# Attention with small batches on one core: scores of a step in one visit, weighted values on quarters of the array, some orders of work changed

## What is computed

```python
W = weights[condition]                                    # per batch element, 32x32
h = einsum('bct,bcd->bdt', x, W)                          # x: (64, 32, 512)
q, k, v = h @ Wq + bq, h @ Wk + bk, h @ Wv + bv           # 512 -> 4096 each
q, k = rms_norm(q, gq), rms_norm(k, gk)                   # over all 4096 columns
attn = softmax(q k^T / sqrt(128))                         # 32 heads of 128, 32 positions
x = x + (attn v) @ Wo + bo                                # 4096 -> 512
...
x = x + ffn(cond2(x))      # a 512x512 quantized weight with a low-rank part, then 8 experts of rank 16
```

## Time and profile before

| what | value |
|---|---|
| median of 3 runs | 1569.63 us (1569.2 to 1571.09) |
| profiled execution | 1569.52 us |
| its span, first to last instruction | 1567.9 us |
| TensorE matmul busy | 1547.8 us, 99% of the span |
| VectorE, ScalarE, GpSimd busy | 1075.9, 709.7, 767.9 us |
| mean granted TensorE clock | 0.997 of full speed |

### The profile page before, as it was taken

How to read it: one execution, slowest core, us unless ns; L and a number is a source line. 1 busy time by engine, 2 the same in 40 slices (tenths; PEclk the granted TensorE clock), 3 DMA queues, 4 the chain that set the end, 5 groups by cost and what they waited for, 6 DMA issues and landing times.

```text
span 1567.9 us, 30891 instructions
## 1 busy us (share of the span) xinstructions
PE 1547.8 (99%) x12566; PEld 1320.7 (84%) x12566; DVE 1075.9 (69%) x1464; ACT 709.7 (45%) x1200; POOL 767.9 (49%) x531
## 2 busy tenths in 40 slices
PE   9999999999999999999999999999999999999998
PEld 8777777777777777777999999998888888888886
DVE  7677677676776767765688888957556655655642
ACT  6666666666666666664333333333332222222210
POOL 6477777777777777764344444424431111111100
PEclk9999999999999999999999999999999999999998
DMA  3111011110011110112333343445452342243220
GB/s 140 55 42 39 26 41 42 42 42 29 34 42 42 42 42 29 35 42 82 120 134 125 134 135 135 145 165 189 155 191 78 89 134 89 93 135 94 81 94 27
DMA packets 105885, 134.33 MB, mean 86 GB/s; under 512 B 6016, under 2 KB 88064, under 8 KB 105232
## 3 DMA queue, kind: packets, MB, share of 16 engines
q1 hardware_dynamic: 105280, 132.23, 25.5%
q10 hardware_dynamic: 464, 0.13, 0.0%
HBM read 86.20 MB, written 46.14 MB: 84 GB/s over the span
## 4 chain that ended last, share of the span: by engine, by line
PE 88%; POOL 4%; DVE 4%; issue 3%; ACT 1%; DMA 1%; POOLq 0%; SPq 0%; DVEq 0%; ACTq 0%
PE bank L558 34%; PE bank L765 22%; PE bank L567 18%; PE bank L720 7%; POOL accr L1194 3%; PE bank L641 3%; PE bank L820 1%; PE bank L803 1%; DVE accr L1375 1%; DMA wraw<-score_spill 1%; PE bank L523 1%; DVE qreg L1374 1%; PE bank L543 0%; POOL wraw L1152 0%; DVE xs_lo L1340 0%
## 5 line engine op out<-in xcount | busy, mean ns | idle before, releaser
L558 PE MATMUL bank<-xs_hi,wa 128*128 128x512 f32 x1792 | 588.8, 398 | 2.2 <-ACT snap L945 1.3
L1194 POOL TENSOR_TENSOR accr<-accr,sqst 128x512 f32<-128x512 f32 x248 | 368.6, 1498 | 172.8 <-ACT sqst L957 112.3
L558 PEld LDWEIGHTS bank<-xs_hi,wa 128*128 128x128 f32 x1792 | 336.3, 188 | 76.3 <-issue 3.8
L558 PE MATMUL bank<-xs_lo,wa 128*128 128x512 f32 x896 | 349.9, 390 | 0.0
L567 PE MATMUL bank<-wv,xs_hi 128*128 128x256 f32 x1792 | 323.9, 284 | 3.9 <-DVE vo L1418 2.1
L765 PE MATMUL bank<-ot,wo_main 128*128 128x512 f32 x1344 | 319.5, 393 | 0.6 <-DVE accr L1605 0.6
L765 PEld LDWEIGHTS bank<-ot,wo_main 128*128 128x128 f32 x1344 | 248.3, 188 | 49.8 <-issue 0.8
L567 PEld LDWEIGHTS bank<-wv,xs_hi 128*128 128x128 f32 x1792 | 279.3, 192 | 6.6 <-issue 3.1
L567 PE MATMUL bank<-wv,xs_lo 128*128 128x256 f32 x896 | 253.5, 283 | 0.0
L1279 DVE TENSOR_TENSOR wa<-wraw,wa 128x256 fp32r<-128x256 f32 (+1 forms) x160 | 170.4, 1066 | 87.3 <-ACT wa L868 86.9
L1594 DVE SCALAR_TENSOR_TENSOR ot<-bank,vec,ot 128x512 fp32r<-128x512 f32 x128 | 95.0, 750 | 185.6 <-ACT ot L1088 177.8
(11 more groups left out here) (184 smaller groups left out, 1757.4 us busy)
## 6 DMA issues: line engine op xcount, KB each, us to landing
sqst<-v_spill SPq DMA_DIRECT2D x63, 512.0 KB, 3.9
wraw<-in_wqk SPq DMA_DIRECT2D x32, 512.0 KB, 3.3
v_spill<-vo SPq DMA_DIRECT2D x64, 256.0 KB, 2.3
v_spill<-sqst SPq DMA_DIRECT2D x64, 256.0 KB, 2.4
score_spill<-sqst SPq DMA_DIRECT2D x32, 256.0 KB, 2.0
wraw<-in_wv SPq DMA_DIRECT2D x16, 512.0 KB, 4.8
wraw<-score_spill SPq DMA_DIRECT2D x16, 512.0 KB, 5.3
accr<-in_wo SPq DMA_DIRECT2D x16, 512.0 KB, 4.7
```

The source lines that it names most:

```text
L558: ins = pe.matmul(dst[:, :], wa[:, col:col + P], xpart[:, j - 1, kt, n * CH:(n + 1) * CH], start=(first and k == 0), stop=(k == 5), skip_g ...
L1194: pool.tensor_tensor(a, a, sq_slot(count), ALU.add).then_inc(acc_done, 1)
```

## The change

- Scores: `scores_lo` and `scores_hi` become one `scores(s)`, which does all 32 matmuls of a step one after the other into one bank, 3 or 7 by the step's parity. It stands behind p7. VectorE's two copies become one of 128x256.
- Products: from step 1 on, p1 of the next step comes before p7 rather than after it. ScalarE's `split_qk(1, h + 1)` moves ahead of the wait for p4. At the end of stage 1 the scores of step 63 stand behind p5 and p6 of the first step of stage 2.
- Weighted values: `pv(b)` does both heads in one go on quarters of the array. Each 128x128 matmul becomes four of 64 rows by 64 columns of the array with 64 moving columns: row half r reads partitions 64r to 64r+63 and writes bank 4 + r, column half d writes partitions 64d to 64d+63. The parts of `pt` that are always zero are no longer multiplied. It waits until all of the step before has been taken out (`o_lo` at 2b).
- Taking out: `out_hi(b, r)` and `out_lo(b, r)` go by bank; each is two instructions of 128x256, one per head.
- Entry of stage 3: `pv(0)` stands between p7 and p4; its taking out moves ahead of the last copies of stage 2; of `project_out(0)` outputs 3 and 2 come before `pv(1)` and 0 and 1 after it.
- Chunk changes: VectorE's `residual` moves from p = 1, ahead of the transposes, to p = 0, behind `out_lo` and ahead of `shift`.
- End: `low_rank_last` runs over the four residual tiles in the outer loop and starts on each as it is done.

```diff
-        def pv_bank(b, h):
-            return bank[4 + (2 * b + h) % 3]
+
+        pv_bank = (bank[4], bank[5])
+
+        def pv_part(r, h):
+            return pv_bank[r][:, h * 256:(h + 1) * 256].rearrange("p (t n) -> p t n", t=TC)
+
+        def ot_part(o, r):
+            return o.rearrange("p (t r n) -> p r t n", t=TC, r=2)[:, r]
...
+            def scores(s):
+
+                dst = bank[3 + 4 * (s % 2)]
+                if s >= 2:
+                    pe.wait_ge(kept, s - 1)
+                if s in (4, 5):
+                    pe.wait_ge(lora_used, s - 3)
                 pe.wait_ge(gq_lo, s + 1)
                 pe.wait_ge(c21_done, s + 1)
-                if s == 3:
-                    pe.wait_ge(lora_used, 1)
-                elif s >= 1:
-                    pe.wait_ge(kept_lo, s)
-                batches(bank[3], blk["q_lo", s % 2], blk["k_lo", s % 2]).then_inc(s_lo, 1)
-
-            def scores_hi(s):
                 pe.wait_ge(gq_hi, s + 1)
                 pe.wait_ge(c22_done, s + 1)
-                if s == 3:
-                    pe.wait_ge(lora_used, 2)
-                elif s >= 1:
-                    pe.wait_ge(kept_hi, s)
-                batches(bank[7], blk["q_hi", s % 2], blk["k_hi", s % 2]).then_inc(s_hi, 1)
+                for i, part in enumerate(("lo", "hi")):
+                    q, k = blk["q_" + part, s % 2], blk["k_" + part, s % 2]
+                    for t in range(TC):
+                        for j in range(NB):
+                            cols = slice(t * P + j * C, t * P + (j + 1) * C)
+                            at = (i * TC + t) * C
+                            ins = pe.matmul(dst[j * C:(j + 1) * C, at:at + C], q[:, cols], k[:, cols],
+                                            start=True, stop=True)
+                ins.then_inc(scored, 1)
...
                     mix(3)
+                    p7(s)
+                    p1(s + 1)
                 else:
                     p6(s)
                     p5(s)
-                    scores_lo(s - 1)
-                if s == 4:
-                    pe.wait_ge(kept_hi, 3)
-                    lora(1)
-                p7(s)
-                p1(s + 1)
+                    p1(s + 1)
+                    p7(s)
+                    scores(s - 1)
                 p2(s + 1)
-                if s == 3:
+                if s in (3, 4):
                     pe.wait_ge(ld_quant[0], 48)
-                    pe.wait_ge(kept_lo, 3)
-                    lora(0)
+                    pe.wait_ge(kept, s)
+                    lora(s - 3)
                 p4(s)
-                if s >= 1:
-                    scores_hi(s - 1)
                 p3(s)
...
+            def pv(b):
+                pe.wait_ge(ld_v[b % 2], 16 * (b // 2 + 1))
+                pe.wait_ge(pt_ready, b + 1)
+                if b >= 1:
+                    pe.wait_ge(o_lo, 2 * b)
+                else:
                     pe.wait_ge(c21_done, N_ST - 1)
-                elif q == 1:
                     pe.wait_ge(c12_done, N_ST - 1)
-                else:
-                    pe.wait_ge(c11_done, N_ST - 1)
-                for t in range(TC):
-                    ins = pe.matmul(pv_bank(b, h)[:, t * P:(t + 1) * P], values(b)[:, t, h * DH:(h + 1) * DH],
-                                    pt[:, b % 2, h, t, :], start=True, stop=True)
+                for h in range(2):
+                    for t in range(TC):
+                        for d in range(2):
+                            for r in range(2):
+
+                                rows = slice(r * 64, (r + 1) * 64)
+                                out = pv_bank[r][d * 64:(d + 1) * 64, (h * TC + t) * 64:(h * TC + t + 1) * 64]
+                                ins = pe.matmul(out, values(b)[rows, t, h * DH + d * 64:h * DH + (d + 1) * 64],
+                                                pt[rows, b % 2, h, t, r * 64:(r + 1) * 64], start=True, stop=True)
                 ins.then_inc(pv_done, 1)
...
-            scores_lo(N_QK - 1)
             p5(N_QK)
-            scores_hi(N_QK - 1)
             p6(N_QK)
+            scores(N_QK - 1)
...
-                    pv(0, 1)
+                    pv(0)
                 p4(s)
                 p3(s)
...
-            def project_out(b):
+            def project_out(b, outputs=range(KI)):
                 c, p = b // NP, b % NP
                 if c == 0:
                     pe.wait_ge(wo_lo, p + 1)
                 pe.wait_ge(o_lo, 2 * b + 2)
-                for i in range(KI):
+                for i in outputs:
...
+            def low_rank_last():
+
+                c = NCH - 1
+                pe.wait_ge(fin_done, KI * c)
+                for i in range(KI):
+                    pe.wait_ge(res_done, KI * c + i + 1)
+                    for t in range(TC):
+                        ins = pe.matmul(job_bank(c, t // 2)[:, (t % 2) * LR:(t % 2 + 1) * LR],
+                                        xr[c % 2][:, i, t * P:(t + 1) * P], lowmat[:, i, :],
+                                        start=(i == 0 and t % 2 == 0), stop=(i == KI - 1), skip_group_check=True)
+                        if i == KI - 1 and t % 2 == 1:
+                            ins.then_inc(rl_done, 1)
...
-                if b >= 1:
-                    pv(b, 0)
-                    pv(b, 1)
+                if b == 1:
+                    project_out(0, (3, 2))
+                    pv(1)
+                    project_out(0, (0, 1))
+                elif b >= 2:
+                    pv(b)
                     project_out(b - 1)
...
                 square(sq_k_hi(s), 1, s % 2 + 2, blk["k_hi", s % 2], None)
+                if s % 2 == 0 and s >= 2 and h + 1 < H:
+                    split_qk(1, h + 1)
                 act.wait_ge(p_done[4], s + 1)
...
+            def out_hi(b, r):
+                act.wait_ge(pv_done, b + 1)
...
+                for h in range(2):
+                    ins = act.activation(ot_part(ot[:, b % 2, 0, h, :], r), pv_part(r, h), ACT.Identity,
+                                         bias=vec[:, 2 * (b % NP) + h, 2:3], scale=1.0)
+                ins.then_inc(o_hi, 1)
...
+                if s == N_ST - 1:
+                    for r in range(2):
+                        out_hi(0, r)
                 act.wait_ge(p_done[4], s + 1)
...
+            def keep_scores(s):
+                h = s // 2
+                dve.wait_ge(scored, s + 1)
+                if s == 0:
                     dve.wait_ge(t_lo, 16)
+                if s % 2 == 0 and h >= 2:
                     dve.wait_ge(spilled[h % 2], 16 * (h // 2))
+                dst = stage[:, h % 2, :].rearrange("p (a m n) -> p m a n", a=2, m=2)[:, s % 2]
+                dve.tensor_copy(dst, bank[3 + 4 * (s % 2)][:, 0:2 * TC * C].rearrange("p (a n) -> p a n", a=2))\
+                   .then_inc(kept, 1)
...
+            def out_lo(b, r):
+                dve.wait_ge(o_hi, 2 * b + r + 1)
+                if b == 0:
+                    dve.wait_ge(p_done[4], N_ST)
+                for h in range(2):
+                    ins = dve.scalar_tensor_tensor(out=ot_part(ot[:, b % 2, 1, h, :], r), in0=pv_part(r, h),
+                                                   scalar=vec[:, 2 * (b % NP) + h, 2:3],
+                                                   in1=ot_part(ot[:, b % 2, 0, h, :].bitcast(F32), r),
+                                                   op0=ALU.add, op1=ALU.subtract)
+                ins.then_inc(o_lo, 1)
...
+                if u == 31:
+                    out_lo(0, 0)
+                    out_lo(0, 1)
...
-                if c >= 1 and p == 1:
-                    residual(c - 1)
                 if 1 <= b < STEPS - 1:
                     transpose_p(b + 1)
-                out_lo(b, 0)
-                out_lo(b, 1)
+                if b >= 1:
+                    out_lo(b, 0)
+                    out_lo(b, 1)
+                if c >= 1 and p == 0:
+                    residual(c - 1)
```

105 lines of the change are left out of this document (28 added, 77 removed).

## The result

The changed kernel takes 1523.63 us (median of 4 runs, 1521.82 to 1525.24); the kernel before took 1570.18 us beside it (4 runs). The ratio is 0.9703 [0.9687, 0.972]: faster by 3%. The profiled execution took 1523.46 us with a span of 1521.7 us, where the one of before had 1567.9 us: 46.2 us less, where the prediction's sum had 57.4 us.

What follows compares the result with a forecast made beforehand. TensorE was taken to bound the kernel, its matmuls busy for 1547.8 of 1567.9 us. The terms summed to 1569.5 - 21.1 - 34.6 - 0.9 - 0.8 = 1512.1 us, with a range from 1500 to 1546 us (0.83).

Steps and rivals of the forecast that it cites:

- What bounds the kernel: Whole kernel: time is a sum of TensorE's intervals, matmuls busy 1547.8 of 1567.9 us; other engines matter only through waits.
- Scores in one visit: Stage 1: merging two scores visits saves one fixed part, 0.34 us a step, 21.1 us over 62 steps.
- fixed part not shared: Rival, scores visits: the records cost the 0.34 us, not the division change; saves 13.6 us or less, 1520 us; chance 0.05.
- What the re-ordering makes late: Stage 1: low weights needed 2.7 us into a step, not 4.7; slack 0.7 us in two-level steps; cost nothing.
- End of stage 1: First wait grows to some 3 us, second goes; together 0, between -1.5 and +2 us.
- Weighted values on quarters: Stage 3: four quarters at once, 14 ns a record, visit 1.24 us; saves 0.54 us in 64 visits, 34.6 us.
- two at a time: Rival, stage 3 quarters: records 27.8 ns apart, visit 2.12 us, 1568.5 us, no change; chance 0.09 with cases near it.
- One by one: Rival, stage 3 quarters: records 55.6 ns apart, 2.12 us more a visit, 1682 us, slower; chance 0.06.
- Taking out is late: Rival, stage 3: halves cost nearly a whole, 0.69 and 0.75 us; 8 + 3 us lost, 1523 us; chance 0.08.
- The page's rule of 60 cycles: Contrary rule, quarter matmuls: about 60 cycles (25 ns) each whatever the columns; visit 1.9 us, some 1557 us.
- Taking out, chunk changes: Stage 3: taking out hidden, 0; at chunk changes residual wait goes, o_lo 0.3 to 0.5 us late; 0, from -0.9 to +2.
- Entry and end: Stage 3 entry: gains 0.9 us, most of the second wait returning one visit later; end: low-rank product gains 0.8 us.

Runs made afterwards that it cites:

- two_visits: The changed kernel with the scores in two visits a step again (lo behind p7, hi behind p4), still one bank and one copy: 1548.49 us.
- doubled: The changed kernel with every record of the scores and weighted-values visits done twice within the same visit: 1622.15 us.
- levels_odd: The changed kernel with VectorE's second levels moved to odd steps (7, 27, 43 in place of 8, 26, 44): 1519.04 us in one run.
- whole_64col: The changed kernel with weighted values on the whole array, 128 stationary and 64 moving columns a record: 1662.24 us.
- row_halves: The changed kernel with the array divided by rows only for the weighted values, 128 stationary and 64 moving columns a record: 1575.49 us.
- rows_in_turn: The changed kernel with the same quarter matmuls, all of the upper rows before all of the lower: 1569.36 us.
- p7_first: The changed kernel with p7 back ahead of the next step's p1, scores in one visit behind both: 1515.6 us, ratio 0.9656; run again, 1518.24 us.

## Why the prediction was right, and where its sum was off

The time, 1523.6 us, is in the range and faster, as forecast; the likeliest case was the right one, with four quarters side by side, and its sum was 11.5 us too low.

- **What bounds the kernel**: right. TensorE is busy for 99%, and each gain is an interval of its own that became shorter.
- **Scores in one visit**: the mechanism is right and the size nearly. 0.34 us a step was forecast. The plain step is 0.286 us shorter (0.33 in executions with steps of 10.42 us, but the one trace of before has the wider starts behind its visits too, so 0.29 compares like with like), and *two_visits* gives back 0.29. Over 61 steps it is 17.5 us instead of 21.1. *doubled* shows that the fixed part isn't a matter of the records, against the rival *fixed part not shared*.
- **What the re-ordering makes late**: the step that failed in stage 1. I gave the low weights 0.7 us on VectorE; in an even step with two levels they took 1.67 us, and the slack of 0.7 us was gone. The trace of before could have told: there the same instruction takes 1.36 us and more in 33 of its 64 executions, and the earlier trace rows shows one of the short ones. GpSimd and VectorE in the kernel before, then in the changed one:

```profile
303.03 1.29 POOL L1194 TENSOR_TENSOR accr<-accr,sqst 128x512 f32<-128x512 f32 x1 [0.93 <-ACT sqst L959]
303.50 1.36 DVE L1279 TENSOR_TENSOR wa<-wraw,wa 128x512 fp32r<-128x512 f32 x1 [1.10 <-ACT wa L868]
...
318.95 2.07 POOL L1204 TENSOR_TENSOR accr<-accr,sqst 128x512 f32<-128x512 f32 x1 [0.16 <-ACT sqst L963]
```

  In both traces the low weights began while GpSimd was adding squares, and ended 0.55 us behind the end of that instruction. So do all 33 long ones of before and all seven of 1.66 us in the changed kernel, to within 0.01 us; the short ones began when GpSimd was idle or had 0.11 us or less of an instruction left. That GpSimd is what holds them up is read from these times; no run takes its sums away.

  The price was inside what the prediction named for it (less than 1 us for each of three steps): 0.28 us each, 0.85 in all, gone in *levels_odd*. Not foreseen was the wait of 1.16 us in the first steps, where the low weights stand behind the small operations of the quantization on VectorE; I had looked only at one steady step. Step 3, in which that wait lies, is 1.36 us longer than before (13.39 and 12.03), where 0.34 less was forecast. With the 3.6 us of the visit, 1.7 at step 3, 0.2 at step 4 and 0.8 of the long steps this is the 6.3 us that steps 1 to 61 miss; the head start of 0.8 us makes it 5.5.
- **End of stage 1**: forecast 0, between -1.5 and +2; measured -2.3, outside the bounds. The first wait grew to 2.91 us as forecast (some 3 us). The second one went, as forecast, but waits of 0.60 us for the next low weights and 0.77 us at the norm sums came in its place. And the price of a wait isn't its length alone: the clock at 0.50 behind it added 1.2 us. Without that the term was inside its bounds: *levels_odd*, with the same waits and the clock at 1.00, loses 0.8 us in this stretch. No row of before shows a fall behind a wait: behind its longest, 2.52 us, the clock stayed.
- **Weighted values on quarters**: four at a time is right, and the size close. 14.95 ns and 0.34 us fixed where 14 and 0.34 were taken: a visit of 1.30 instead of 1.24 us, 64 x 0.06 = 3.8 us of the sum, nearly all that stage 3 missed; the rest are the chunk changes. The reason was only half right. I divided the price of the moving columns; *whole_64col* and *row_halves* show that it is the load of the stationary columns. The change halves both, so the number came out the same by either; that part was luck. A change that cuts only the moving columns would have been forecast badly.
- **Rivals**: *two at a time* falls for the changed kernel, and *rows_in_turn* shows its 27 ns a record in another loop order. *One by one* (55.6 ns) falls. *Taking out is late* falls although its time, 1523 us, is nearly the measured one: halves take 474 and 478 ns, and TensorE meets no wait for them in ordinary steps. A time that agrees is no proof; the steps of 6.76 us are. *Fixed part not shared* gave 1520 us and falls by *doubled* and *two_visits*.
- **The page's rule of 60 cycles** ("TensorEngine Tiling (Array Packing)" of the Trainium skill, Instruction Overhead), an estimated 25 ns a matmul and 1557 us: this case disagrees, with 8.9 and 14.95 ns between the starts of records. A matmul of the program leaves two records, so counted by these it is 17.8 ns in the scores, still below 25, and 29.9 in the weighted values, above it.
- **Taking out, chunk changes**: the taking out is hidden in ordinary steps, as forecast. At the first change the wait of 1.03 us for the output taken out is twice what I named (0.3 to 0.5 us); the shift ahead of it waits for scores, a transfer that took 11.12 us:

```profile
1144.52 11.12 DMA wraw<-score_spill
```

  With the slow first matmuls behind it this change costs 1.10 us over a plain step (7.86 and 6.76), where the kernel before lost 0.88 (8.12 and 7.24). At the next two the steps are 6.91 us, 0.15 more than a plain one, where before lost nothing. So the term that I had at 0 was -0.5.
- **Entry and end**: 2.4 us to the third visit where 0.9 and two visits, 2.0 in all, were forecast, with the wait of 1.32 us one visit later, where the prediction put it; 1.7 where 0.8 and a visit were.

## What to carry to other kernels

Find out what a small matmul is bound by, its moving or its stationary columns: only a tile that makes the binding one smaller helps, and consecutive matmuls must go to different tiles, rows and columns alternating (1.16 us against 1.91 us for the same 64 records). Gather small matmuls of another division into one visit, as each visit has a price of its own (0.3 us here) apart from its records. When work is put ahead of other work, look at the first and last steps too, and at every execution of an instruction that it waits for, not at one (0.69 and 1.36 us here). Give a long wait of TensorE a range above its length, since the clock may drop behind it. Before a difference of 1 or 2 us in 1500 is put down to an edit, run the same code again.

## What the runs showed of the hardware that was not expected

- A record with 128 stationary columns costs 110 ns with 64 moving columns and 111 ns with 128. Loads of tiles on other rows and on other columns overlap: 55.7 ns with two row halves, 26.9 with two column quarters on the same rows, 14.95 with all four quarters. A load's record is 192 ns with 128 stationary columns, 188 with half of the rows, 134 with 64 columns and 110 with 32.
- A VectorE instruction of 0.69 us (128x512, f32 to fp32r) took 1.10 to 1.67 us where it began while GpSimd was adding 128x512 tiles, and ended 0.55 us behind GpSimd's instruction. That one causes the other was not tested.
- Behind 2.91 us of waiting, in which TensorE was busy for 0.78 of 3.60 us, the granted clock was 0.50 (1.2 GHz) for the next 3.1 us; behind 2.94 us in *levels_odd*, 1.07 us in *p7_first* and 2.52 us in the kernel before it stayed at 1.00. So the length of the wait alone doesn't decide it. At the end of the program, 1.70 us of work in 5 us were followed by a stretch at 0.59; with matmuls in the gaps it was 1.00.
- Two lengths of the same step, 10.42 and 10.46 us, in executions of the same code and within one (*levels_odd*), at a granted clock of 1.00. The cause stays open.
